# Reciprocals in a 128x128 tile, key projections between raw products, constant rows kept in the stacks, and query stacks ahead of the mask pieces, in a two-layer cross-attention kernel

## What is computed

```python
# layer 0: x (16,512,256), ctx_1024 (16,1601,256), mask (16,512,1601)
Q = split_heads(x @ Wq.T + bq); K, V = ctx_1024 with Wk, bk and Wv, bv
scores = einsum('bhqd,bhkd->bhqk', Q, K) / sqrt(16)
scores = where(mask[:, None] == 0, -1e9, scores)
ctx = einsum('bhqk,bhkd->bhqd', softmax(scores), V)
x = layer_norm(merge(ctx) @ Wo.T + bo + x)
# layer 1
h = x + mamba2(rms_norm(x))              # 8 heads of 64, state 128, 4 taps
q = (layer_norm(h) @ Wq); k = ctx_1024 @ Wk; v = ctx_1024 @ Wv
out = h + merge(softmax(q k^T / sqrt(32)) v) @ Wo
```

## Time and profile before

| what | us |
|---|---|
| median of 3 executions | 9346.83 (9342.91 to 9347.22) |
| the profiled execution, device time | 9338.74 |
| its span | 9336.7 |
| PE busy | 7945.1 (85%) |
| VectorE (DVE) busy | 5175.2 (55%) |
| ScalarE (ACT) busy | 3325.7 (36%) |
| GpSimd (POOL) busy | 1900.6 (20%) |
| mean granted clock of TensorE | 0.88 |

### The profile page before, as it was taken

How to read it: one execution, slowest core, us unless ns; L and a number is a source line. 1 busy time by engine, 2 the same in 40 slices (tenths; PEclk the granted TensorE clock), 3 DMA queues, 4 the chain that set the end, 5 groups by cost and what they waited for, 6 DMA issues and landing times.

```text
span 9336.7 us, 126518 instructions
## 1 busy us (share of the span) xinstructions
PE 7945.1 (85%) x36866; PEld 3514.3 (38%) x36866; DVE 5175.2 (55%) x12793; ACT 3325.7 (36%) x4038; POOL 1900.6 (20%) x1759
## 2 busy tenths in 40 slices
PE   4988888897888979889888898888889888897888
PEld 1343433334333343433434334343343433334343
DVE  4566465565655556455563656646556565555645
ACT  1424334242342424324243342433424234242432
POOL 3030220402113031130302203022040211303113
PEclk6989889898997979989798898988989899897998
DMA  4131331413204042131322313133141320404213
GB/s 81 20 68 31 46 56 20 70 28 57 52 12 77 21 65 44 22 70 24 68 35 41 60 20 66 32 46 55 20 70 28 57 52 12 77 21 65 44 21 70
DMA packets 217075, 425.44 MB, mean 46 GB/s; under 512 B 35797, under 2 KB 126839, under 8 KB 216067
## 3 DMA queue, kind: packets, MB, share of 16 engines
q1 hardware_dynamic: 216399, 417.03, 26.5%
HBM read 194.50 MB, written 8.51 MB: 22 GB/s over the span
## 4 chain that ended last, share of the span: by engine, by line
PE 54%; issue 15%; DVE 13%; DMA 8%; POOL 5%; SPq 3%; ACT 1%; DVEq 0%; POOLq 0%; ACTq 0%
PE ps L939 13%; PE ps L876 10%; PE ps L910 7%; PE ps L912 7%; DMA stage<-in_mask 5%; DVE mx L1497 5%; PE ps L944 4%; PE ps L857 3%; PE ps L914 3%; DVE rs L1510 2%; PE ps L895 2%; DMA KS<-const_krows 1%; PE ps L1054 1%; DVE xc L1609 1%; PE ps L1204 1%
## 5 line engine op out<-in xcount | busy, mean ns | idle before, releaser
L1281 ACT ACTIVATE PR<-ps 128x1024 f32<-128x1024 f32 x2496 | 2501.3, 1023 | 3177.1 <-PE ps L912 1691.1
L1468 DVE CUSTOM_DVE_ANT_0 ps<-ps,maskq 128x402 f32<-128x402 f32 x4201 | 2412.5, 587 | 1685.4 <-PE ps L876 1544.5
L876 PE MATMUL ps<-KS,QS 96*128 96x402 bf16 x4201 | 1464.1, 357 | 360.2 <-DVE mx L1468 261.7
L939 PE MATMUL ps<-PR,vbuf 128*32 128x512 f32 x9984 | 1376.9, 624 | 5.1 <-ACT PR L1281 5.1
L910 PE MATMUL ps<-QS,KS 99*128 99x512 bf16 x3328 | 1286.7, 387 | 15.1 <-DVE xres L1693 14.9
L912 PE MATMUL ps<-maskk,identb 128*128 128x512 bf16 x3328 | 1281.9, 385 | 0.0
L876 PEld LDWEIGHTS ps<-KS,QS 96*128 96x128 bf16 x4201 | 402.7, 99 | 1984.8 <-DVE mx L1468 1301.4
L1497 DVE TENSOR_REDUCE mx<-ps 128x2 f32<-128x804 f32 x1024 | 930.6, 987 | 305.7 <-PE ps L895 305.6
L895 PE MATMUL ps<-KS,QS 97*128 97x402 f32 x2048 | 818.6, 543 | 181.6 <-DMA QS<-const_krows 96.6
L670 POOL TENSOR_TENSOR khl<-rest,khl 128x402 fp32r<-128x402 f32 (+1 forms) x128 | 123.2, 962 | 3392.3 <-ACT rest L1247 3392.3
L914 PE MATMUL ps<-QS,KS 99*128 99x512 f32 x1664 | 757.6, 530 | 20.7 <-DVE small L1494 10.9
(11 more groups left out here) (179 smaller groups left out, 6970.9 us busy)
## 6 DMA issues: line engine op xcount, KB each, us to landing
KS<-khl SPq DMA_DIRECT2D x402, 200.1 KB
KS<-khl SPq DMA_DIRECT2D x96, 800.5 KB
stage<-in_maskt SPq DMA_DIRECT2D x204, 256.0 KB
stage<-in_mask SPq DMA_DIRECT2D x204, 201.0 KB
ctxs<-in_ctxt SPq DMA_DIRECT2D x17, 1601.0 KB, 16.8
QS<-qhl SPq DMA_DIRECT2D x402, 64.0 KB
QS<-q1hl SPq DMA_DIRECT2D x96, 256.0 KB
win_s<-in_w_in SPq DMA_DIRECT2D x16, 1288.0 KB, 5.7
```

The lines of the kernel that those rows point to most:

```text
L876: pe.matmul(ps[:, bank, 0:w], QS[gi][0:KROWS, h, i * P:(i + 1) * P], KS[gi][0:KROWS, h, c0:c0 + w], start=True, stop=True).then_inc(s_raw, 1)
L939: mm = pe.matmul(ps[32 * j:32 * j + 32, 6, :], l, PR[:, t % 2, j, :], start=(t == 0), stop=(t == KT - 1), tile_position=(0, 32 * j))
L1281: nc.scalar.activation(PR[:, t % 2, 2 * half:2 * half + 2, :], ps[:, 2 * half:2 * half + 2, :], ACT.Exp, scale=scale).then_inc(s_p, 1)
L1468: nc.vector.tensor_tensor_reduce(src, src, maskq[:, i, c0:c0 + w], 1.0, -3.0e38, ALU.add, ALU.max, mx[:, c, h * QT + i:h * QT + i + 1]).th ...
```

## The change

Four edits.

1. **Sums.** Four small products gather the sums of a group's four query tiles into a 128x128 tile of PSUM bank 7 (`sums`, with `pick0` for layer 0 and `pick1` for layer 1), VectorE inverts that tile (`inverse`), four products with `sel` spread it over the partitions (`spread`, slots 0 to 3 of step 1), and VectorE multiplies from PSUM (`normalize`). `divide` stays for the first layer-1 group. The two out-projections are cut in two: the groups but the last go between the spreads, the last group after `normalize`.
2. **Key projections as entries.** The four `BACK` projections become entries ("back") among the raw products of group 1, and the turn of the second layer-1 group becomes an entry ("turn1") beside the first layer-1 group. The list has 265 entries; by place they are 61, 52, 62, 50, 40 and 0. In the last layer-1 group steps 0 and 1 have none, and the projections fall on slot 4 of steps 6 to 9.
3. **Constant rows.** The slots become parts of two persistent tiles, `kst` and `qst`. Their constant rows are loaded once, at the start; layer 1's lie in rows 96 to 99 and GpSimd sets three rows of `qst` to 0 in each batch. Only group 0's stack still loads them.
4. **Order.** SP issues the query stacks ahead of mask pieces 2 to 5. GpSimd converts pieces 0 and 1 ahead of `FRONT`'s parts and 2 to 29 behind. The forward projections all run inside the raw stage, after units 7, 14, 21, 28, 35 and 41.

```diff
-        CUTS = [(0, 56, 0, KT - 1)], [(56, FIRST1, 0, 3), (FIRST1, 106, 4, KT - 1)], [(106, 164, 0, KT - 1)], \
-               [(164, 218, 0, KT - 1)], [(218, NENT, 0, KT - 4)], []
-        BACK_STEP = 4
+        CUTS = [(0, 61, 0, KT - 1)], [(61, FIRST1, 2, 4), (FIRST1, FIRST1 + 48, 5, KT - 1)], \
+               [(FIRST1 + 48, FIRST1 + 110, 0, KT - 1)], [(FIRST1 + 110, FIRST1 + 160, 1, KT - 1)], \
+               [(FIRST1 + 160, NENT, 1, KT - 4)], []
...
+                if gi == 0 and k == 7:
+                    ENTRIES.append(("turn1", 1, 0))
...
+                if gi == 1 and k in BACK_AT:
+                    ENTRIES.append(("back", 0, BACK_AT.index(k)))
...
-        PIECE0, PIECE1, PIECE2, PIECE3 = 2, 6, 10, 14
+        PIECE1, PIECE2, PIECE3 = 2, 10, 14
...
-        FRONT_FIRST, FRONT_EVERY = 3, 8
+        FRONT_EVERY = 7
...
-                sp.dma_start(KS[gi][KROWS:SROWS, :, :], krows.rearrange("r (h s) -> r h s", h=GH))\
-                    .then_inc(s_stack[gi], 16)
...
-                load_pieces(b, bn, 0, PIECE0, False)
                 load_xt(bn)
+                load_pieces(b, bn, 0, PIECE1, False)
...
                 load_ctx(bn)
-                load_pieces(b, bn, PIECE0, PIECE1, False)
                 for g in range(G1):
                     stack_q1(b, g)
...
+            def sums(b, gi):
...
+                for i in range(QT):
+                    mm = pe.matmul(ps[32 * i:32 * i + 32, 7, 0:P], pk[:, :], src[:, i * P:(i + 1) * P], start=True, stop=True,
+                                   tile_position=(0, 32 * i))
+                mm.then_inc(s_sum, 1)
+
+            def spread(b, gi, i):
...
+                r = slice(32 * i, 32 * i + 32)
+                pe.matmul(ps[:, 7, i * P:(i + 1) * P], sel[r, :], rsm[r, :], start=True, stop=True,
+                          tile_position=(32 * i, 0)).then_inc(s_spread, 1)
...
                 def between(t, slot):
-                    if pos == 1 and (t, slot) == (BACK_STEP, 0):
-                        back()
+                    if t == 1 and 0 < gi < G0 and slot < QT:
+                        spread(b, gi - 1, slot)
...
-                for _ in range(FRONT_FIRST):
-                    forward()
...
+                sums(b, NG - 1)
+                project_out(wo1_s, 0, G1 - 1, G1, NG - 1)
                 pe.wait_ge(s_norm, LEAD + b * NG + NG)
...
+                project_out(wo1_s, G1 - 1, G1, G1)
...
+            def inverse(b, gi):
...
+                nc.vector.reciprocal(rsm[:, :], ps[:, 7, 0:P]).then_inc(s_rs, 1)
```

More of the change, by code:

```diff
@@ L407, in xattn_mamba @@
         assert sorted(e for a in beside for x in a.values() for e in x) == list(range(NENT))
-        ALONE0 = [e for a in beside[:2] for x in a.values() for e in x]
-        assert ALONE0 == list(range(len(ALONE0)))
+        ALONE0 = [e for a in beside[:2] for x in a.values() for e in x if ENTRIES[e][0] != "turn1"]
+        assert len(ALONE0) == max(ALONE0)
+        BACK_STEPS = {t: [ENTRIES[e][2] for slot in range(SLOTS) for e in beside[1].get((t, slot), ())
+                          if ENTRIES[e][0] == "back"] for t in range(KT)}
         ENTRIES1 = [("raw", 0, k) for k in range(UNITS)]
         ENTRIES1 += [("raw", 1, k) for k in range(4)] + [("turn", 0, 0)]
-        ENTRIES1 += [("raw", 1, k) for k in range(4, UNITS)] + [("turn", 1, 0)]
+        ENTRIES1 += [("raw", 1, k) for k in range(4, UNITS)]
         NSETS = 3
-        assert len(ENTRIES1) == NENT1 and NENT1 % NSETS == 0
+        assert len(ENTRIES1) == NENT1
         def raw1_place(k):
@@ L858, in project, with left @@
                 mm.then_inc(s_proj, 1)
+            def left(b, e):
+                while e >= 0 and ENTRIES[e][0] == "turn1" and isinstance(b, int):
+                    e -= 1
+                if e < 0:
+                    pe.wait_ge(s_rawfree, LEAD + b * NCOUNT)
+                elif ENTRIES[e][0] == "back":
+                    pe.wait_ge(s_rest, rests(b, BACK[ENTRIES[e][2]]) + 1)
+                elif ENTRIES[e][0] == "turn1":
+                    pe.wait_ge(s_mrow1, b * G1)
+                else:
+                    pe.wait_ge(s_rawfree, LEAD + b * NCOUNT + counted[e] + 1)
             def entry(b, e):
@@ L1273, in exponentials @@
                 for t in range(KT):
-                    if gi == G0 + 1 and t == BACK_STEP:
-                        for j, item in enumerate(BACK):
-                            take(b + 1, item, 4 + (FIRST1 + j) % 2)
+                    if gi == G0 + 1:
+                        for j in BACK_STEPS[t]:
+                            take(b + 1, BACK[j], 4 + ENTRIES.index(("back", 0, j)) % 2)
                     act.wait_ge(s_pv, LEAD + b * NG * KT + max(gi * KT + t - 1, 0))
@@ L1294, in _ @@
                 take(0, item, pj_bank[item])
-            for n, item in enumerate(BACK):
-                take(0, item, 6 + n % 2)
+            for j, item in enumerate(BACK):
+                take(0, item, 4 + ENTRIES.index(("back", 0, j)) % 2)
             with act.Fori(0, B) as b:
@@ L1519, in group @@
                     for slot in range(SLOTS):
-                        if t == 0 and slot == GH and gi not in (0, G0):
+                        if slot == GH and 0 < gi < G0:
+                            if t == 0:
+                                inverse(b, gi - 1)
+                            elif t == 1:
+                                normalize(b, gi - 1)
+                        elif slot == GH and gi > G0 and t == 0:
                             divide(b, gi - 1)
```

246 lines of the change are left out of this document (153 added, 93 removed).

## The result

The changed kernel took **9559.07 us** in the median (9510.51 to 9599.96, 4 executions) against 9346.17 in the same session: ratio 1.0226, 95% interval 1.0171 to 1.0281. I had forecast 9294 with a range of 9165 to 9430, and faster. The profiled execution took 9599.96 us, the longest of the four, against 9338.74 of the one before. The kernel's own spread of 0.9% is new too: before, the executions lay within 0.05%.

A forecast was written before the change was run, and what follows sets the result against it. PE was taken as busy nearly throughout both layers' groups, idle in five places. Terms -8.9 + 0 - 4.0 - 6.6 + 0.9 + 15.3 gave -3.3 us a batch, -53 over 16: 9294 us, range 9165 to 9430.

The forecast's parts named there:

- Step 5: Layer-1 raw stage: query stacks first start products 6.6 us sooner, but late mask conversions move its end +15.3 us.
- The sign that I had named: First layer-1 group's start: VectorE's first raw reduction waits some 20 us for GpSimd's mask conversions, new in each batch.
- Step 2: End of layer 0: variance and out-projection timing unchanged, GpSimd's memsets covered by its wait; 0, bounds -1 and +1.
- Step 1: Layer-0 groups: 128x128 sums tile shortens the reciprocal and PE's wait; -8.9 us a batch, bounds -11 and -5.
- Step 3: Batch end: shorter chain of sums, tile and spreads at full clock instead of half; -4.0 us a batch.
- the alternative: Batch end: PE at half clock throughout, gaining only 0.5 us.
- Step 4: Last layer-1 group: key projections as entries replace a block, -6.6 us, bounds -10 and 0; group before +0.9.
- Start: Prologue: interleaved projections gain some 7 us, waiting for ten constant-row transfers loses as much; 0.
- A: Last layer-1 group: projections as entries buy nothing, group stays at 69.6 us; +106 in all, 9400; chance 0.24.
- C: Layer-0 groups 1 and 2 above 50 us: PE waits 2 us for the tile; +67, 9361; with the like 0.09.
- My sum: Whole kernel: all terms together, -3.3 us a batch, 9294 us; own range 9215 to 9375, chance 0.58.

The follow-up runs named there:

- run 1: Changed kernel, but GpSimd converts mask pieces 0 to 5 ahead of the forward projections' parts: 9423.83 us, ratio 1.0077.
- run 2: Changed kernel with mask pieces 0 to 5 converted first and forward projections every 4 units instead of 7: 9206.63 us, ratio 0.9841.
- run 3: Kernel before the change, with only the change's new order of query stacks, mask pieces and forward projections: 9626.53 us, ratio 1.0298.
- run 5: Changed kernel with one layer-1 key projection put back ahead of layer 0's out-projection: 9488.16 us, ratio 1.0147.
- run 8: Changed kernel with GpSimd's two 3x2048 memsets moved from behind layer 0's variance to behind the query stack's pad: 9558.31 us, ratio 1.0227.
- run 6: Changed kernel with spreading products over the full 128x128 array instead of 32 rows, and pick0 for both layers: 9344.12 us, ratio 0.9993.
- run 7: Changed kernel with 55 entries beside the first layer-1 group instead of 61, ten in steps 0 to 4 of the second: 9501.07 us, ratio 1.0170.
- run 11: Changed kernel with six pieces first, projections every 4 units, full-array spreads, memsets between pieces 1 and 2, entries table edited, GpSimd's start unblocked: 8932.64 us, ratio 0.9547.

## Why the prediction was wrong

By its own steps, us a batch, forecast and measured:

| step | forecast | measured |
|---|---|---|
| 1. sums in the tile, groups 0 to 3 | -8.9 | -2.4 |
| 2. end of layer 0, with norm and Mamba | 0 | +7.0 |
| 3. batch's end | -4.0 | -1.1 |
| 4. projections as entries, last group | -6.6 | -3.2 |
| 4. and 5. the group before, and the order | +0.9 +15.3 | +14.4 |
| once, at the start | 0 | +21 |

**Step 5, which I called the term that decides, was right,** in mechanism and in size. The first masked reduction came 96.6 us behind the first half of the queries (4774.29 - 4677.68), where I had 99.5 (5786.6 - 5687.1); 41.1 us from the last part to the last query piece, forecast 41.3. The raw products started 4 us sooner than I thought. Runs 1, 2 and 3 show that the wait is the order's doing: half of it comes from the pieces (run 1), half from the projections (run 2). The sign that I had named, a wait of VectorE for the mask of some 20 us, is there with 23.04.

**Step 2 failed worst:** 0 forecast, 7.0 measured. "The same PE work stands before it" priced the work and not the clock it runs at. PE is given small products on few rows and waits of 0.72 and 1.17 us just where a key projection used to stand; it falls to 1.2 GHz and does the out-projection there. That is 5.6 us a batch by the one batch that kept its clock, and run 5 takes all of it away. In the same step I had set the memsets at nothing because GpSimd waited 6.83 us. GpSimd had the time, but VectorE, which GpSimd was waiting for, paid: run 8, which moves the memsets alone, takes 2.0 us out of the norm's stretch. Most of the rest of its 3.3 is no loss but a shift: one key projection that used to run ahead of the out-projection now runs behind it, and GpSimd takes the variance 6.7 us after the out-projection's end instead of 5.1. Step 2 alone would have turned my -3.3 into a loss, but it does not carry the result by itself: with it at 0, the misses of steps 1, 3 and 4 (6.5, 2.9 and 3.4 us, against 1.8 that step 5 stayed under its forecast) still leave +7.6 a batch and the start's 21.

**Step 1's spread was too cheap.** I took 0.2 us for each spread, from columns alone; it costs 0.41 in a group as built and 0.22 with all 128 rows (run 6). The reciprocal was right: 0.96 measured, 0.95 from the straight line, PE waiting 0.54 where I had 0.6. As built groups 1 to 3 take 50.6, 49.1 and 40.6 us, with full-array spreads 49.1, 48.1 and 39.3, where I had 47.5, 47.7 and 39.1; the 1.6 that group 1 is still off I have not traced.

**Step 3** had named the alternative that mostly came true, half clock at the end, with a gain of 0.5 instead of 4.2; I then gave it hardly any weight and took 4.0. It gained 1.1: 12.8 after, 10.7 with full-array spreads, 9.9 forecast. My parts also add up to a gain of 4.8 and not 4.2.

**Step 4** was right in its price: steps 6 to 9 take 7.0 to 7.4 us in the mean where I said 6.8. What was missing is step 1, 1.3 us more at a lower clock for want of entries (run 7), and the group's end: its last three steps take 15.8 us instead of 13.7 in the tenth batch, at a clock of 1.00 in both kernels, since 18 raw products stand there instead of 14. The wait for group 1's stack comes to 0.4 by my own figures (15.8 against 15.4), not 0.8.

**Start.** I let gain and loss cancel without a row. GpSimd waited 16 us for transfers that it did not need yet (nine of them; I had counted ten), and run 11 has 16.6 of the 21 back.

Of the rivals none came true by its mechanism. A said slower because of the entries' steps, and they were near their price. C's sign, a group above 50, showed in group 1, but its cause, a wait of 2 us for the tile, did not: it is 0.54. My sum had only terms of waiting and of counted columns, so everything that was not in it had one sign. With step 5 at +15 the gain hung on a few small gains of uncertain size, all of them on PE's side, and a chance of 0.34 for slower was too low. The sum's own range was too narrow as well: it is 5 us a batch either way, where the bounds of steps 4 and 5 alone allow 7.7 down and 10.3 up.

## What to carry to other kernels

Price a product by the clock at which it will run: taking a large product out of a stretch with waits can cost more than the wait that the edit removes. Before something urgent is moved forward in a queue, list what it pushes back on each in-order engine and who waits for that; a work item that others need later is best put into the engine's idle time ahead of the new work, and the trace shows where that is. An operation on an idle engine is not free if it shares a port with the one everybody waits for.
